# Logits of four tiles at once, second-half tiles stored turned, routing counts later, four residual additions on GpSimd

## The chip, the cores and the metric

The kernel runs on one core of a Trainium2 chip. The metric is the device time of one execution in microseconds. Before the change three runs took 824.46, 827.03 and 829.4 us; the median is 827.03 us.

## What is computed

The input is 2 x 1024 tokens of 512 numbers. Two residual blocks follow one another, each as `x + layernorm(f(layernorm(x)))`. The first f is attention (local windows, and global rows for the 62 largest queries and the two end tokens of each head). The second is a mixture of experts over all T = 2048 tokens, and this is the part that the change touches:

```
xt = layernorm(x).reshape(T, 512)
probs = softmax(xt @ Wg)                  # 8 experts
eidx = argmax(probs); gate = probs[eidx]
oh = one_hot(eidx, 8)
pos = (cumsum(oh, axis=0) * oh).sum(-1) - 1
keep = pos < 256                          # capacity
xd[eidx * 256 + pos] = xt                 # where keep
h = silu(xd @ W1) * (xd @ W3); oe = h @ W2          # per expert, H = 704
out = take(oe, ...) * (gate * keep)
shared = silu(xt @ sw1) * (xt @ sw3) @ sw2
x = x + layernorm(out + shared)
```

## The kernel before

Tokens are worked on in 16 tiles of 128. Matrix products in fp32 accuracy are made of a high and a low part of each operand (`split`, L169: a copy to the high part, on ScalarE, and a subtraction for the low part, on VectorE, `tt` L149) and three matmuls (`product3`, L286). The program builds one list of instructions for each engine, and each engine runs its list in order; semaphores tie them together. The order of the calls in the Python code is therefore the order in every list. SyncE issues most DMAs, also in order; indirect DMAs stand in GpSimd's list, between its arithmetic.

After the attention comes a list of passes (L1481): two of the shared expert for tokens 0 to 1023 (q = 0 and 1, 512 tokens each), eight experts (q = 2 to 9, 256 rows each), and two of the shared expert for tokens 1024 to 2047 (q = 10 and 11). A pass has `up` (L1324) with six blocks m = 0 to 5 (24 matmuls each, 12 in the last) and `down` (L1358), in which tiles 0 and 1 go through m = 0 to 5 as a pair and then tiles 2 and 3. A `step(m)` is called behind each block of `up`, and `between(t0, m)` behind each block of `down`. PSUM banks of `up` come from a ring of four (`UP`), those of `down` from a ring of two (`DN`), which ScalarE empties into `OUTR` (L1382). The logits use a single bank (`MSC`).

**Second layernorm and routing.** `work()` (L1556) is one step n of a software pipeline over the tiles. In step n it calls, for the tile that many steps back, `h_logits` (5 back, the matmuls with Wg), `h_turn` (4 back: four transposes on TensorE, then a copy or a split), `h_h2` (3 back: L934 on VectorE, then an activation on ScalarE), `h_mean2` (2 back), `h_x1` (1 back, with an addition on GpSimd at L874) and `h_mean` (0 back). Both means end in a power on GpSimd (L284). Step 7 stands ahead of q = 0, steps 8 to 12 behind its blocks m = 0 to 4, steps 13 to 15 in its `down`, steps 16 to 21 behind the blocks of q = 1. When four tiles have logits, `route_count` (L1416, 12 to 14 small VectorE operations) runs in the same step, right behind the logits and ahead of the step's other functions; one step later `route_place` (L1446) makes eight small matmuls, nine small VectorE operations and four indirect scatters on GpSimd into `scr_xd`. The experts' passes read `scr_xd` back in `prepare` (L1484), turn the rows on TensorE (`turned`, L915) and split them.

**Logits.** For tiles 0 to 7 `h_logits` makes eight matmuls per tile, with the turned 128 x 128 tile as the stationary operand and Wg (high and low, 16 columns) as the moving one. For tiles 8 to 15 it makes four matmuls in plain fp32 (eight records in the trace), with 8 columns.

**Second half.** `h_h2` stores the rows of tiles 8 to 15 to `scr_h` (`h2d`), and `prepare` loads them before q = 10 and 11 and turns them: four transposes a tile, at blocks m = 2 to 5 of q = 9 and q = 10.

**Last additions.** In q = 10 and 11, `step(m)` calls `conclude(m - 2)` (L1543: a tensor_scalar, the residual addition and the store of the result), then `combine(m - 1)` (L1531: a scalar_tensor_tensor of the gathered expert row and the shared row, then the statistics and GpSimd's power), then `fetch(m)` (L1512: an indirect gather on GpSimd and two loads). Tiles 0 to 3 are concluded in q = 10, tiles 4 to 7 in q = 11, tiles 8 to 15 at the ends of the two.

## Time and profile before

| | |
|---|---|
| median of three runs | 827.03 us (824.46 to 829.4) |
| the profiled execution, its own time | 822.52 us |
| its span, first to last instruction | 820.8 us |
| TensorE busy | 776.2 us (95%) |
| VectorE busy | 563.0 us (69%) |
| ScalarE busy | 422.9 us (52%) |
| GpSimd busy | 146.1 us (18%) |
| mean granted clock of TensorE | 0.992 of 2.4 GHz |

In the rows, PE is TensorE, DVE VectorE, ACT ScalarE, POOL GpSimd, SPq the DMA queue of SyncE. A row of the timeline has the start in us from the start of the span, the duration, the engine, the source line, the operation and output<-inputs; in brackets stands how long the engine was idle before it and what it waited for. XT, WQL and WKL hold turned tiles (WQL and WKL are old weight buffers used again), SIL and HH the hidden layer, STC the statistics of a tile, LG the routing's small operands, XX and CX the residual and the shared row. Small helpers (L145, L149, L163, L167) carry most operations, so tiles tell them apart.

### The profile page before, as it was taken

How to read it: one execution, taken by the hardware profiler on the slowest of the kernel's cores; microseconds unless marked ns; L12 is line 12 of the kernel's file. 1: busy time of each engine (PE TensorE's matmuls, PEld its weight loads, DVE VectorE, ACT ScalarE, POOL GpSimd, SP SyncE). 2: the span in 40 equal slices, each digit the busy share in tenths (PEclk: the TensorE clock that was granted, in tenths of full speed). 3: DMA queues.
4: the chain of work that ended last, by engine and by line, in shares of the span. 5: the costliest groups of instructions: out<-in, count | busy, mean ns of one | idle time of the engine just before them, and what ended most of it. 6: DMA issues, size and time to landing. Idle time of an engine off the chain costs nothing.

```text
span 820.8 us, 13876 instructions
## 1 busy us (share of the span) xinstructions
PE 776.2 (95%) x5060; PEld 650.2 (79%) x5060; DVE 563.0 (69%) x1196; ACT 422.9 (52%) x839; POOL 146.1 (18%) x227
## 2 busy tenths in 40 slices
PE   6998999989999999998999999999999999999994
PEld 4786777777777777776878887999999999887883
DVE  5764798468888566777588545466776666758666
ACT  5464352445656565767544244566675666633120
POOL 3300010510111113332354432000000000013122
PEclk9999999999999999999999999999999999999998
DMA  7789565976775888872349622676778776546444
GB/s 233 230 275 346 167 187 168 276 199 174 190 202 156 204 215 234 230 198 92 105 149 312 233 98 94 186 230 200 219 237 237 227 237 221 171 146 204 138 155 141
DMA packets 117492, 162.39 MB, mean 198 GB/s; under 512 B 17364, under 2 KB 65236, under 8 KB 117424
## 3 DMA queue, kind: packets, MB, share of 16 engines
q1 hardware_dynamic: 113840, 153.54, 61.9%
q0 software_dynamic: 3584, 7.97, 3.3%
q8 instruction: 40, 0.66, 0.4%
q14 instruction: 28, 0.23, 0.1%
HBM read 107.24 MB, written 55.05 MB: 198 GB/s over the span
## 4 chain that ended last, share of the span: by engine, by line
PE 63%; DVE 19%; DMA 6%; ACT 5%; issue 4%; SPq 1%; POOL 1%; POOLq 0%; DVEq 0%; ACTq 0%
PE bank L163 40%; PE wide L163 17%; DVE MX L160 4%; PE wide L167 3%; PE bank L167 2%; DVE SG L160 2%; DMA XX<-scr_xd 2%; DMA scr_q<-hl 1%; DVE STC L281 1%; ACT PTG L145 1%; DVE GC L153 1%; DMA H2A<-scr_oe,FG 1%; DMA scr_qtok<-H2A 1%; DVE TV L744 1%; ACT PT L157 1%
## 5 line engine op out<-in xcount | busy, mean ns | idle before, releaser
L163 PE MATMUL wide<-W2H,HH 128*128 128x512 f32 x308 | 101.9, 396 | 0.5 <-ACT OUTR L145 0.5
L160 DVE TENSOR_REDUCE MX<-wide 128x1 f32<-128x192 f32 (+1 forms) x128 | 77.6, 646 | 19.4 <-PE wide L163 19.3
L157 ACT ACTIVATE PT<-bank 128x512 f32<-128x512 f32 x128 | 73.6, 593 | 28.5 <-PE bank L163 28.4
L157 ACT ACTIVATE SIL<-bank 128x256 f32<-128x256 f32 (+1 forms) x72 | 32.7, 454 | 97.8 <-PE bank L163 97.6
L149 DVE TENSOR_TENSOR SIL<-bank,SIL 128x256 f32<-128x256 f32 (+1 forms) x72 | 36.8, 511 | 63.8 <-ACT SIL L157 63.2
L163 PE MATMUL bank<-XT,W13H 128*128 128x256 f32 (+1 forms) x336 | 76.6, 322 | 0.0
L145 ACT ACTIVATE HH<-SIL 128x256 fp32r<-128x256 f32 (+1 forms) x72 | 35.2, 489 | 67.5 <-DVE SIL L149 67.5
L163 PEld LDWEIGHTS wide<-W2H,HH 128*128 128x128 f32 x308 | 58.5, 190 | 13.2 <-ACT OUTR L145 1.3
L149 DVE TENSOR_TENSOR HH<-SIL,HH 128x256 fp32r<-128x256 f32 (+1 forms) x72 | 37.0, 514 | 45.5 <-ACT HH L145 37.3
L163 PE MATMUL wide<-W2L,HH 128*128 128x512 f32 x168 | 66.6, 396 | 0.9 <-DVE W2L L149 0.7
L163 PEld LDWEIGHTS bank<-XT,W13H 128*128 128x128 f32 x336 | 55.0, 188 | 4.7
L163 PE MATMUL bank<-WQL,W13H 128*128 128x256 f32 (+1 forms) x168 | 55.3, 329 | 0.0
L163 PE MATMUL bank<-WQL,W13L 128*128 128x256 f32 (+1 forms) x168 | 54.3, 323 | 0.0
L163 PE MATMUL bank<-WKL,W13H 128*128 128x256 f32 (+1 forms) x168 | 54.3, 323 | 0.0
L284 POOL TENSOR_TENSOR STC<-STC,mhalf 128x1 f32<-128x1 f32 x48 | 29.0, 604 | 138.4 <-DVE STC L153 135.1
L163 PE MATMUL bank<-XT,W13L 128*128 128x256 f32 (+1 forms) x168 | 53.6, 319 | 0.0
L1516 POOL DMA_INDIRECT H2A<-scr_oe,FG x8 | 8.0, 997 | 210.7 <-issue 210.7
L149 DVE TENSOR_TENSOR W13L<-R,W13H 128x512 fp32r<-128x512 f32 x70 | 44.1, 685 | 1.7 <-ACT W13H L145 1.7
L163 PE MATMUL bank<-XT,WQH 128*128 128x256 f32 (+1 forms) x192 | 43.0, 319 | 0.0
L163 PE MATMUL bank<-WVH,HT 128*128 128x512 f32 x128 | 41.1, 410 | 1.0 <-ACT HT L145 0.7
L149 DVE TENSOR_TENSOR W2L<-R,W2H 128x512 fp32r<-128x512 f32 x60 | 41.2, 686 | 1.3
L163 PE MATMUL bank<-HT,WKH 128*128 128x512 f32 x128 | 41.1, 402 | 0.0
(253 smaller groups left out, 2007.5 us busy)
## 6 DMA issues: line engine op xcount, KB each, us to landing
R<-in_L_ffn_W_dram SPq DMA_DIRECT2D x48, 512.0 KB, 5.5
scr_q<-hl SPq DMA_DIRECT2D x16, 512.0 KB, 4.3
scr_k<-hl SPq DMA_DIRECT2D x16, 512.0 KB, 4.1
R<-in_L_ffn_sw_dram SPq DMA_DIRECT2D x12, 512.0 KB, 5.3
QSe<-scr_q SPq DMA_DIRECT2D x36, 128.0 KB, 3.6
KSe<-scr_k SPq DMA_DIRECT2D x36, 128.0 KB, 3.0
scr_v<-vt SPq DMA_DIRECT2D x16, 272.0 KB, 2.2
R<-_attn_hidden_states_dram SPq DMA_DIRECT2D x16, 256.0 KB, 3.8
```

The costliest lines, as they stand in the source:

```text
L145: return do(e, lambda g: g.activation(dst, src, ACT.Copy), after)
L149: return do(e, lambda g: g.tensor_tensor(dst, a, b, op), after)
L153: return do(e, lambda g: g.tensor_scalar(dst, a, s1_, None, op0), after)
L157: return do("act", lambda g: g.activation(dst, src, fn, **kw), after)
L160: return do("dve", lambda g: g.tensor_reduce(dst, src, AXX, op), after)
L163: return do("pe", lambda g: g.matmul(ps, a, b, start=start, stop=stop, skip_group_check=True), after, mark=mark)
L167: return do("pe", lambda g: g.transpose(ps, a, idn), after, mark=mark)
L281: a = do("dve", lambda g: g.bn_stats(st[:, 8:14], src), after)
L284: return do("pool", lambda g: g.tensor_tensor(st[:, 2:3], st[:, 3:4], mhalf[:, :], ALU.pow), [a, m_half])
L744: m = do("dve", lambda g: g.max(v8, N_[:, :]), prev)
L1516: mg = dma("pool", ga_slots[i], lambda e: e.indirect_dma_start(out=gb, out_offset=None, in_=oed, in_offset=bass.IndirectOffsetOnAxis(ap=FG ...
```

## The change

- For tiles 0 to 7 the logits are made by `logits_group`: eight matmuls for four tiles, with Wg's 16 columns stationary and 512 tokens moving, into a bank of `UP`; ScalarE copies the 16 x 512 result to a buffer of `XL`. `logits_fold`, later, adds high and low part and turns the result back with four plain fp32 matmuls (16 rows, 8 columns), into `MSC`. The ScalarE copy and the VectorE addition at the head of `route_count` become one VectorE copy.
- Groups stand in steps 7 and 12, folds in step 8 and behind block m = 5 of q = 0. Counts: in step 8 behind the other functions, behind m = 5 of q = 0, and in steps 16 and 20, behind the others. Places: step 10, at (0, 3) in `down` of q = 0, step 18, and behind m = 5 of q = 1.
- `down` of q = 0 holds four steps (13 to 16, at (0, 1), (0, 4), (2, 1), (2, 4)) where it held three; q = 1 holds steps 17 to 21 behind m = 0 to 4.
- Tiles 8 to 15 are stored to `scr_h` after their turn, from `XL`, so `prepare` only loads and splits them for q = 10 and 11; no transposes there. A buffer of `XL` (two) is free again when that store has landed.
- In `conclude` the residual addition of tiles 0 to 3 goes to GpSimd.

```diff
+                            m_wg.append(tt(fold[:, :], ident[0:2 * E, 0:E], ident[0:2 * E, E:2 * E], ALU.add, [m_id]))
@@ h_h2: the store of tiles 8 to 15 goes
-            if t >= 8:
-                r0 = (t - 8) * P
-                m = dma("sp", h2s[t % 2], lambda g: g.dma_start(h2d[r0:r0 + P, :], dst),
-                        [m_h] + h2_marks[-2:-1])
-                h2_marks.append(m)
-                h2free[t % 8].append(m)
@@ h_turn, tiles 8 to 15
+                r0 = (t - 8) * P
+                m = dma("sp", h2s[t % 2], lambda g: g.dma_start(
+                    h2d[r0:r0 + P, :], d["dst"][:, :, :].rearrange("p k t -> p (k t)")), d["s"] + h2_marks[-2:-1])
+                h2_marks.append(m)
+                XL.busy[d["li"]].append(m)
@@
+            def logits_group(g4):
+                ui, ps, fr = UP.take()
+                li, lt, lf = XL.take()
+                x_ = xt[g4]
+                for l in range(2):
+                    for k in range(4):
+                        m_l = mm(ps[0:2 * E, :], wghl[:, k, :, :].rearrange("p l e -> p (l e)"),
+                                 x_["b"][l][:, k, :], k + l == 0, k + l == 4, x_["ready"] + m_wg + fr, mark=(k == 3 and l == 1))
+                XT.busy[x_["i"]].append(m_l)
+                m_c = copy("act", lt[0:2 * E, :, :].rearrange("p k t -> p (k t)"), ps[0:2 * E, :], [m_l] + lf)
+                UP.busy[ui].append(m_c)
+                route["lt"] = (li, lt, m_c)
+
+            def logits_fold():
+                li, lt, m_c = route["lt"]
+                route["mi"], route["mb"], fr = MSC.take()
+                for j in range(4):
+                    m_l = mm(route["mb"][:, j * 16:j * 16 + E], lt[0:2 * E, j, :], fold[:, :], True, True,
+                             [m_c] + m_wg + fr, mark=(j == 3))
+                XL.busy[li].append(m_l)
+                route["m_l"] = m_l
@@ route_count
-                if g4 < 2:
-                    a = copy("act", LG[:, 0, :, :], lg[:, :, 1, :], [m_l, m_cum])
-                    a = tt(LG[:, 1, :, :], lg[:, :, 0, :], LG[:, 0, :, :], ALU.add, [a])
-                else:
-                    a = copy("dve", LG[:, 1, :, :], lg[:, :, 0, :], [m_l, m_cum])
+                a = copy("dve", LG[:, 1, :, :], lg[:, :, 0, :], [m_l, m_cum])
@@ prepare
-                    m_t, s = turned(xb, d_["b"], (n - 2) * P, [m_], d_["free"], TPC)
-                    XX.busy[xi].append(m_t)
+                    c = (n - 2) * P
+                    if job < 9:
+                        m_t, s = turned(xb, d_["b"], c, [m_], d_["free"], TPC)
+                        XX.busy[xi].append(m_t)
+                    else:
+                        s = split(d_["b"][0][:, :, c:c + P], d_["b"][1][:, :, c:c + P],
+                                  xb[:, :].rearrange("p (k t) -> p k t", k=4), "act", [m_] + d_["free"])
+                        XX.busy[xi] += s
@@ conclude
-                m_f = tt(xb[:, :], xb[:, :], cb, ALU.add, [m_n, mx_])
+                m_f = tt(xb[:, :], xb[:, :], cb, ALU.add, [m_n, mx_], e="pool" if t < 4 else "dve")
@@ work
+            PLACE_AT = {10: 0, 18: 2}
                 if n == 7:
-                    h_logits(0)
-                    h_logits(1)
+                    logits_group(0)
+                if n == 8:
+                    logits_fold()
+                if n == 12:
+                    logits_group(1)
                 for back, fn in ((5, h_logits), (4, h_turn), (3, h_h2), (2, h_mean2), (1, h_x1), (0, h_mean)):
                     t = n - back
-                    if 4 <= t < 16 or 0 <= t < 4 and fn is h_logits:
+                    if (8 if fn is h_logits else 4) <= t < 16:
                         fn(t)
-                        if fn is h_logits and t % 4 == 3:
-                            route_count(t // 4)
-                if n % 4 == 1 and 9 <= n <= 21:
-                    route_place(n // 4 - 2)
+                if n in (8, 16, 20):
+                    route_count((n - 8) // 4)
+                if n in PLACE_AT:
+                    route_place(PLACE_AT[n])
@@ step
-                    if q == 1 or q == 0 and m < 5:
+                    if q == 0 and m == 5:
+                        logits_fold()
+                        route_count(1)
+                    if m < 5 and q < 2:
                         work()
+                    if q == 1 and m == 5:
+                        route_place(3)
@@ between
-                        if q == 0 and (t0, m) in ((0, 2), (2, 0), (2, 4)):
+                        if q == 0 and (t0, m) in ((0, 1), (0, 4), (2, 1), (2, 4)):
                             work()
+                        if q == 0 and (t0, m) == (0, 3):
+                            route_place(1)
```

## Rows read from the trace of the kernel before

**Rows 1.** The page: busy time, share of the span and instructions

```profile
PE 776.2 (95%) x5060; PEld 650.2 (79%) x5060; DVE 563.0 (69%) x1196; ACT 422.9 (52%) x839; POOL 146.1 (18%) x227
```

**Rows 2.** Timeline of TensorE: its longer idle times in brackets

```profile
171.91 0.48 PE L163 MATMUL bank<-QSe,KSe 97*128 97x256 f32 x2 [1.11 <-DVE vt L149]
...
412.83 1.03 PE L163 MATMUL wide<-wghl,XT 128*128 128x16 f32 x8 [1.02 <-DVE STC L934]
...
449.50 0.50 PE L163 MATMUL wide<-W2H,HH 128*128 128x512 f32 x1 [0.23 <-ACT OUTR L145]
...
497.66 0.18 PE L163 MATMUL bank<-OHB,trib 128*128 128x8 bf16 x1 [0.73 <-DVE OHB L146]
498.55 0.18 PE L163 MATMUL bank<-CUMB,onesb 128*128 128x8 bf16 x1 [0.71 <-DVE CUMB L146]
...
754.62 0.47 PE L163 MATMUL wide<-W2L,HH 128*128 128x512 f32 x1 [0.70 <-DVE W2L L149]
```

**Rows 3.** Windows: busy us per engine, then PEclk, DMA share, GB/s

```profile
410.00:420.00 10.00, 8.98 (x46) 7.18 (x45) 8.80 (x28) 4.18 (x8) 2.54 (x3) 0.83 0.26 86
500.00:510.00 10.00, 9.77 (x36) 7.56 (x35) 6.87 (x20) 6.35 (x11) 4.42 (x4) 0.83 0.13 45
```

**Rows 4.** Chain that ended last: start, us; 24 logit matmuls, 24 of block 0

```profile
396.85 2.63 PE wide L163 x24
399.49 5.58 PE bank L163 x24
```

**Rows 5.** Timeline of VectorE, q = 0: blocks' first operations, L934, place, count

```profile
405.72 0.69 DVE L149 TENSOR_TENSOR SIL<-bank,SIL 128x512 f32<-128x512 f32 x1 [5.05 <-ACT SIL L157]
...
415.14 0.68 DVE L149 TENSOR_TENSOR SIL<-bank,SIL 128x512 f32<-128x512 f32 x1
...
419.61 0.15 DVE L934 SCALAR_TENSOR_TENSOR STC<-STC 128x1 f32<-128x1 f32 x1
...
422.14 0.18 DVE L149 TENSOR_TENSOR LG<-bank,LG 128x32 f32<-128x32 f32 x1
...
423.67 0.68 DVE L149 TENSOR_TENSOR SIL<-bank,SIL 128x512 f32<-128x512 f32 x1
...
440.02 0.18 DVE L149 TENSOR_TENSOR LG<-wide,LG 128x32 f32<-128x32 f32 x1
...
442.44 0.15 DVE L934 SCALAR_TENSOR_TENSOR STC<-STC 128x1 f32<-128x1 f32 x1
```

**Rows 6.** Timeline of ScalarE: the activation behind L934

```profile
448.07 0.82 ACT L157 ACTIVATE H2A<-XX,STC 128x512 f32<-128x512 f32 x1 [0.47 <-DVE STC L934]
```

**Rows 7.** End of q = 1: first load of expert rows, their transposes, landing time

```profile
511.40 0.80 SPq L1503 DMA_DIRECT2D XX<-scr_xd  x2
...
515.53 1.03 PE L167 MATMUL wide<-ident,XX 128*128 128x128 f32 x8
...
XX<-scr_xd SPq DMA_DIRECT2D x3, 256.0 KB, 3.5
```

**Rows 8.** Chain that ended last: a tile's transposes; a combine and the next gather

```profile
743.43 0.44 PE wide L167 x4
...
783.96 0.76 DVE CX L1535
...
786.67 3.40 DMA H2A<-scr_oe,FG
```

**Rows 9.** Timeline of VectorE, q = 10: residual addition and two combines

```profile
735.90 0.69 DVE L149 TENSOR_TENSOR XX<-XX,CX 128x512 f32<-128x512 f32 x1
736.51 0.75 DVE L1535 SCALAR_TENSOR_TENSOR CX<-H2A,GK,CX 128x512 f32<-128x512 f32 x1
...
742.85 0.75 DVE L1535 SCALAR_TENSOR_TENSOR CX<-H2A,GK,CX 128x512 f32<-128x512 f32 x1
```

**Rows 10.** Timeline of GpSimd and VectorE: an addition, a one-column operation beside it

```profile
458.15 1.26 POOL L149 TENSOR_TENSOR XX<-XX,CX 128x512 f32<-128x512 f32 x1
458.21 1.22 DVE L934 SCALAR_TENSOR_TENSOR STC<-STC 128x1 f32<-128x1 f32 x1 [3.62 <-POOL STC L284]
```

More of the change, by code:

```diff
@@ L180, in sandwich @@
         wghl = sb(top, "wghl", [P, 4, 2, E], F32R)
+        fold = sb(top, "fold", [2 * E, E])
         wt8 = sb(top, "wt8", [P, E])
@@ L1393, in sandwich @@
             scat = []
+            def logits_group(g4):
[18 more added lines that the diff above has]
+                route["m_l"] = m_l
             def h_logits(t):
-                g4, j = divmod(t, 4)
+                j = t % 4
                 d = hs[t]
@@ L1399, in h_logits @@
                     route["mi"], route["mb"], route["mfree"] = MSC.take()
-                mb, dst = route["mb"], d["dst"]
-                if g4 < 2:
-                    col = d["col"]
-                    for k in range(4):
-                        for l in range(2):
-                            m_l = mm(mb[:, j * 16:(j + 1) * 16].rearrange("p (l e) -> p l e", l=2),
-                                     dst[l][:, k, col:col + P], wghl[:, k, :, :], k == 0 and l == 0,
-                                     k == 3 and l == 1, d["s"] + m_wg + route["mfree"], mark=(k == 3 and l == 1))
-                    XT.busy[xt[g4]["i"]].append(m_l)
-                else:
-                    for k in range(4):
-                        m_l = mm(mb[:, j * 16:j * 16 + E], dst[:, k, :], wgs[:, k, :], k == 0, k == 3,
-                                 d["s"] + m_wg + route["mfree"], mark=(k == 3))
-                    XL.busy[d["li"]].append(m_l)
+                for k in range(4):
+                    m_l = mm(route["mb"][:, j * 16:j * 16 + E], d["dst"][:, k, :], wgs[:, k, :], k == 0, k == 3,
+                             d["s"] + m_wg + route["mfree"], mark=(k == 3))
+                XL.busy[d["li"]].append(m_l)
                 route["m_l"] = m_l
@@ L1419, in route_count @@
                 lg = mb[:, 0:64].rearrange("p (j l e) -> p j l e", j=4, l=2)
-                if g4 < 2:
-                    a = copy("act", LG[:, 0, :, :], lg[:, :, 1, :], [m_l, m_cum])
-                    a = tt(LG[:, 1, :, :], lg[:, :, 0, :], LG[:, 0, :, :], ALU.add, [a])
-                else:
-                    a = copy("dve", LG[:, 1, :, :], lg[:, :, 0, :], [m_l, m_cum])
+                a = copy("dve", LG[:, 1, :, :], lg[:, :, 0, :], [m_l, m_cum])
                 L = LG[:, 1, :, :]
```

## The prediction

> **What bounds the kernel now.** I read the page first: TensorE is busy 95% of the span [rows 1], so a matmul taken away pays unless another wait takes its place. Then TensorE's idle times behind the attention [rows 2]: the large ones are 1.02 us in block 1 of q = 0, 0.73 + 0.71 us at the end of q = 1 (both behind a count on VectorE) and 0.70 us in q = 10. Then windows [rows 3]: after each of the first two the granted clock averages 0.83 over 10 us, which is about 3.4 us at 1.2 GHz instead of 2.4 and costs 1.7 us. Idle times of 1.11 us earlier [rows 2] brought no such drop. Last the timeline of VectorE in q = 0 [rows 5]: its list fills each step of 7.0 us, in which TensorE has some 6.9 us to do. So in q = 0 VectorE is a second bound, just hidden. The profiled run took 822.52 us and the median is 827.03; I sum changes against the profiled run and add the sum to the median. A measurement here can tell about 0.5% (4.1 us) from no change.
>
> **Logits, TensorE.** A tile's eight matmuls now cost 2.63 / 3 = 0.88 us [rows 4]; eight tiles cost 7.0 us. After: a 512-column matmul takes 5.58 / 24 = 0.23 us [rows 4], so a group costs 1.9 us. No row has stationary operands of 16 columns; if they don't pipeline, up to 0.40 us each (the time of one such matmul), 1.4 us more a group; I take 0.23, since the load is smaller. The fold (four plain fp32 matmuls, two records each) has no row either: between almost nothing and the time of eight small matmuls, 8 x 0.11 = 0.9 us [rows 4]; I take 0.9, the nearest. Sum 5.6 us, a gain of 1.4 us of TensorE time. It is worth that only where TensorE sets the pace.
>
> **q = 0, step by step, against VectorE.** The group ends 0.8 us earlier than the 24 matmuls, so block 0's first VectorE operation comes at 404.9 instead of 405.72 [rows 5]. A step without count or place lasts 415.14 to 422.14 = 7.0 us; a place 1.5 us (422.14 to 423.67), a count 2.4 us (440.02 to 442.44) [rows 5]. L934 of the next tile stands 4.5 us behind the step's start (415.14 to 419.61), and the tile can be turned 1.0 us later, after 0.82 us of ScalarE [rows 5, 6]. The count is now behind the other functions, so tile 5 is no longer late: the wait of 1.02 us goes. But step 9 starts on VectorE only at 404.9 + 7.0 + 2.4 = 414.3, and tile 6 can be turned at 414.3 + 4.5 + 1.0 = 419.8. TensorE, without logits, is there at 417.0 (404.1, then 0.9 fold, two turns of 0.4 [rows 8] and two blocks of 5.6). What is late next is this: 2.8 us idle. The same list gives 1.0 us before tile 7 and 0.9 us before the second group, which needs tile 7's split (433.7). Group, turn, half block and fold then end at 439.7.
>
> Then the moved count. Each 128x512 operation fewer saves 0.6 us (735.90 to 736.51) [rows 9]: one W13L in block 3, two and the XT split in block 4. So its steps end at 436.2 and 441.4, block 5 takes 2.8, and count 1 starts at 444.2. The logits of tile 8 (step 13, now at (0, 1), 442.5) need the one MSC bank, which is free when the count has read it, 0.4 us later: 2.1 us idle. TensorE then reaches the end of (0, 5) at 452.1. In ScalarE's list the step moved to (0, 4) stands ahead of the copy OUTR that frees the `down` bank: turned copy of tile 10 at 451.9, H2A 0.8 us, OUTR 0.6 us (448.07 to 449.50 for both now) [rows 2, 6], so TensorE starts the second pair at 453.3, 1.2 us idle. Before it started at 449.50 with one step (1.2 us) less done [rows 2]: 450.7. **q = 0 loses 2.6 us.** Bounds: a gain of 4.1 us (1.4 work, 1.0 idle, 1.7 clock) if VectorE doesn't hold it, a loss of 5 if each wait is 0.6 us longer. Step 16's matmuls only move from q = 1 to q = 0. The four scatters of a place and GpSimd's power stay in the same order as before and cover step 15 as before.
>
> **End of q = 1.** Count 3 comes a block earlier and its place two blocks later: 1.44 us idle and 1.7 us of clock go. But q = 2 needs rows scattered by place 3. The first VectorE operation of block 5 was held to 498.5 by the count where its input was there at 497.6 (TensorE ended at 496.93); this 0.9 us is all that the scatters gain. The load issued at 511.40 lands 3.5 us later, at 514.9, and was used at 515.53 [rows 7]: 0.6 us slack. **Gain 1.5 us** of 3.1; bounds 0.9 and 3.1. The other 1.6 us become idle time before those transposes.
>
> **Turned stores.** The stores move one function ahead in SyncE's list and wait for a copy instead of an activation of the same step; same bytes. The buffer of XL, then, waits for its store, two steps (over 9 us) old: nothing, or up to 1 us a step if the store is late. Loads for q = 10 and 11 stay, splits read the loaded buffer (same lengths). Four transposes a tile take 0.44 us [rows 8]: **q = 9 gains 1.8 us** on TensorE; those in q = 10 would give another 1.8 and the idle 0.70.
>
> **Additions on GpSimd.** VectorE loses 0.69 us a tile [rows 9], GpSimd gets 1.26 [rows 10]. In q = 10 combine follows combine after 6.34 us [rows 9]; without the addition VectorE would be back after 5.65, but the next gather lands 6.11 us after a combine (783.96 to 790.07) [rows 8]. So the combine waits, GpSimd's addition starts first, and the combine meets it: beside such an addition a one-column VectorE operation with two SBUF inputs took 1.22 us and ended with it, against 0.15 alone [rows 10, 5]. The combine starts at 5.65 + 0.1 (a semaphore) + 1.26 = 7.0 us, 0.65 later than now; twice that, less the first addition's 0.6: W2L of block 5 comes 0.7 us later than now. TensorE then waits 2.9 us there instead of 0.70: **q = 10 loses 0.7** and its 1.8 us of transposes with it. Bounds: -2.5 and +1.3.
> The Trainium skill (SBUF — State Buffer, "Who interferes with whom") says that an instruction with two SBUF inputs and a GpSimd instruction that reads SBUF exclude each other, and that the later one stands still; by it q = 10 loses 0.7, and without it the combine would wait for the gather alone, and q = 10 gain 1.0. The rows agree with the rule; it speaks against this part.
>
> **Clock.** New idle times of 2.8 and 2.1 us in q = 0 and 2.9 us in q = 10 are longer than the one of 1.02 that brought 1.2 GHz [rows 2, 3]. A drop after the first is hidden by VectorE; I count one of the other two, 1.7 us; bounds 0 and 3 drops, 5.1.
>
> **Sum:** 2.6 - 1.5 - 1.8 + 0.7 + 1.7 = +1.7 us; 824.2 against the profiled 822.52, 828.7 against the median.
>
> **Rivals.**
> - *TensorE sets the pace everywhere* (chance 0.10): -4.1 - 1.5 - 1.8 - 2.5 = -9.9, 817.1. For it: 95% busy. Against it: rows 5 and the gather.
> - *Only q = 0 goes as TensorE would* (0.13): -4.1 - 1.5 - 1.8 + 0.7 = -6.7, 820.3. The waits there rest on sums over some 40 us.
> - *The combine beats the addition* (0.14): q = 10 gains 1.0 instead of losing 0.7: 0.0, 827.0. It would need a gather 0.5 us faster.
> - *Slower: the clock drops after each new idle time* (0.20): in the second half of `down` in q = 0, at the start of q = 2 and in q = 10, +5.1 instead of +1.7, so 832.1. It decides where the idle time passes about the 1.02 us of rows 2. For it: both late cases dropped. Against it: 1.11 us earlier did not.
> - *The weights aren't held* (0.03): 0.40 us a matmul, +2.8, mostly under VectorE: about 830.
>
> **How the numbers follow.** My forecast has 0.40: 828.7. Faster by over 0.5%: the first two rivals and little else, 0.25. Slower: the clock rival and a fifth of the forecast's error, 0.25. Same: 0.50. The range, 819.5 to 833.5, takes in the second rival and the clock, and leaves out TensorE everywhere.
>
> **What would show it.** Right: idle of TensorE near 417, 442 and 452 us, the last two put down to MSC's reader and OUTR; no idle at a count's OHB or CUMB; no transposes from scr_h; L1535 lasting or starting late beside GpSimd's additions in q = 10, and W2L idle there over 2 us. Wrong: `down` of q = 0 starting before 438; combines 5.7 us apart in q = 10; a span under 815 us.

## The result and the profile after

The changed kernel takes 829.68 us (median of 20 runs, 826.7 to 836.03), the kernel before 825.2 us (20 runs, the three shown first among them, 821.32 to 829.4): a ratio of 1.0061, 95% interval 1.0044 to 1.0078, so 5.0 us slower. Ratios here are worked out from the single runs, slow ones left out, and can differ by about a per mille from the quotient of the two medians (here 1.0054). The time itself lies 1 us from the forecast of 828.7 and inside the range. The difference does not: I had summed +1.7 us, and my likeliest case was "within 0.5%", where the middle of the interval is beyond 0.5%. (The kernel before is 1.8 us faster in the 20 runs than in the three shown first; that covers part of my miss. It is luck and no merit of the forecast.)

The page of the changed kernel, the line that answers to [rows 1]. TensorE is busy as long as before, although 64 matmul records are gone (more of it ran at half clock, see below); the span is 829.3 us against 820.8:

```profile
PE 777.0 (94%) x4996; PEld 645.9 (78%) x4996; DVE 563.3 (68%) x1193; ACT 423.5 (51%) x839; POOL 150.9 (18%) x231
```

Timeline of TensorE, changed kernel, all the longer idle times behind the attention, for [rows 2]:

```profile
422.63 0.66 PE L167 MATMUL wide<-ident,H2B 128*128 128x128 f32 x4 [3.08 <-ACT H2B L157]
...
442.02 1.12 PE L167 MATMUL wide<-ident,H2A 128*128 128x128 f32 x4 [3.22 <-ACT H2A L157]
...
452.13 1.03 PE L163 MATMUL wide<-wgs,XL 128*128 128x8 f32 x8 [0.19 <-DVE LS L160]
...
461.27 0.51 PE L163 MATMUL wide<-W2H,HH 128*128 128x512 f32 x1 [0.94 <-ACT OUTR L145]
...
522.92 1.33 PE L167 MATMUL wide<-ident,XX 128*128 128x128 f32 x8 [0.16 <-DMA XX<-scr_xd]
...
719.74 0.47 PE L163 MATMUL wide<-W2L,HH 128*128 128x512 f32 x1 [0.75 <-ACT W13H L145]
...
761.81 0.77 PE L163 MATMUL wide<-W2L,HH 128*128 128x512 f32 x1 [3.61 <-DVE W2L L149]
```

The two idle times at a count's OHB and CUMB are gone. In their place stand three of over 3 us: at tile 6 (422.63), at tile 8 (442.02), and at W2L in q = 10 (761.81). The windows behind them, changed kernel, with the columns of [rows 3]; the granted clock is the first number behind POOL's:

```profile
424.00:428.00 4.00, 4.00 (x13) 3.15 (x12) 3.20 (x8) 2.68 (x5) 1.35 (x2) 0.61 0.55 180
440.00:448.00 8.00, 5.97 (x17) 4.60 (x17) 4.39 (x11) 4.22 (x7) 2.24 (x4) 0.57 1.09 366
760.00:764.00 4.00, 2.19 (x5) 1.82 (x6) 2.94 (x6) 0.69 (x2) 2.60 (x3) 0.70 0.48 139
```

A stretch at a clock of 0.61 for 4 us has cost 4 x 0.39 = 1.6 us of TensorE's time at full speed; the second has cost 8 x 0.43 = 3.4 us. Over the whole span the granted clock cost the kernel before 6.7 us in this way and the changed one 11.6; 3.3 and 3.1 us of that lie in the last 15 us of the span, and 1.7 us of the changed one in the attention.

**Where the time went, by stage.** The starts of the first matmul of each `up` and `down` (for q = 0 the first matmul of the logits ahead of it) cut the span in stages. The row "before" has lengths; the others are differences from it, in us. The kernels e1 to e12 are those of the next section. The last stage is taken from a span with one decimal and is good to 0.1 us.

```
kernel   attention  q=0 up  q=0 down  q=1 up  q=1 down  q=2..8    q=9  q=10 up  q=10 down  q=11 down on  span
                                                                                 + q=11 up
before      396.66   42.88     20.44   38.76     19.47  171.12  25.37    32.15      47.02         26.93  820.8
after        +2.31   +7.08     +2.34   -3.00     -1.21   -0.55  -0.93    -1.66      +4.33         -0.21  829.3
e1           +0.82   +1.63     +5.39   -2.99     -1.19   -0.32  -0.91    -1.64      +4.78         +0.03  826.4
e2           +0.57   +1.10     +4.09   -3.00     -1.14   -0.39  -0.93    -1.64      +4.38         +0.16  824.0
e3           -0.65   +4.00     +4.03   -3.00     -1.11   -0.55  -0.94    -1.66      +1.62         -0.94  821.6
e4           +0.61   +3.21     -0.24   +0.01     -0.03   -0.65  -0.94    -1.65      +1.93         -0.55  822.5
e5           +7.90   +5.17     -0.30   +0.04     -1.64   -0.51  +1.47    +0.02      +2.76         +0.39  836.1
e6           +5.24   +1.58     +1.81   -3.00     +0.17   -0.62  -0.08    +0.00      +0.01         +0.19  826.1
e7           +3.79   +5.01     +1.19   -2.99     -1.14   +0.76  -0.94    -1.65      +1.65         -0.78  825.7
e8           +2.69   -1.20     -0.23   +0.00     -1.47   -0.86  +0.40    +0.01      -0.01         +0.17  820.3
e9           +0.16   +5.94     +2.54   -2.99     -0.66   -0.31  -0.94    -1.64      +3.00         +0.70  826.6
e10          -0.63   +4.34     +4.02   -3.00     -1.23   -0.57  -0.94    -1.65      -0.24         -1.30  819.6
e11          +1.62   -0.01     +1.80   -3.03     +0.12   -0.37  -0.94    -1.65      -0.22         -1.32  816.8
e12          +5.84   +3.15     +1.10   -2.80     -1.64   -0.15  -0.93    -1.65      -0.26         -0.76  822.7
```

The attention is the same code in all of them, and so are q = 2 to 8: these columns, from -0.65 to +7.90 and from -0.86 to +0.76, are what one profiled execution can be off by. The profiles of e5 and e12 are of the slowest of their runs. I compare the other stages and trust the medians for the whole. The ratios have intervals of about 2.5 per mille to either side, so a difference of less than 3 to 4 per mille between two of them is not firm. For the changed kernel: q = 0 costs 9.4 us more, q = 1 4.2 us less (1.2 us of that is the step moved to q = 0), q = 2 to 9 1.5 us less, q = 10 and what follows 2.5 us more.

**What holds tile 8.** ScalarE's timeline in the changed kernel, and GpSimd's, the scatter of tile 0:

```profile
441.16 0.81 ACT L157 ACTIVATE H2A<-XX,STC 128x512 f32<-128x512 f32 x1 [5.64 <-DMA scr_xd<-H2A,FSI]
```

```profile
433.38 1.04 POOL L1478 DMA_INDIRECT scr_xd<-H2A,FSI  x1 [1.02 <-DVE SIL L149]
```

Tile 8's rows go into the buffer of tile 0 (`h2_tile(t)` goes by t % 8), so the activation waits until the scatter of tile 0 has read it. Place 0 moved from step 9 to step 10; the scatter was issued at 424.40 before and at 433.38 now, and among the weight loads of block 3 it took until 441.1, 7.7 us (6.1 us before). I had not followed this edge.

**q = 10.** VectorE's and GpSimd's timelines in the changed kernel, for [rows 9]:

```profile
741.82 0.75 DVE L1551 SCALAR_TENSOR_TENSOR CX<-H2A,GK,CX 128x512 f32<-128x512 f32 x1
...
749.44 0.75 DVE L1551 SCALAR_TENSOR_TENSOR CX<-H2A,GK,CX 128x512 f32<-128x512 f32 x1 [1.93 <-DMA H2A<-scr_oe,FG]
...
755.57 1.43 DVE L1551 SCALAR_TENSOR_TENSOR CX<-H2A,GK,CX 128x512 f32<-128x512 f32 x1 [0.49 <-DMA H2A<-scr_oe,FG]
```

```profile
741.99 1.73 POOL L149 TENSOR_TENSOR XX<-XX,CX 128x512 f32<-128x512 f32 x1 [3.08 <-DVE CX L154]
...
755.16 1.29 POOL L149 TENSOR_TENSOR XX<-XX,CX 128x512 f32<-128x512 f32 x1 [2.02 <-DVE CX L154]
```

The exclusion is there in both directions: at 741.82 the combine starts first and GpSimd's addition takes 1.73 us instead of 1.26 [rows 10]; at 755.57 the addition is under way and the combine takes 1.43 us and ends half a microsecond after it. The combines come 7.6 and 6.1 us apart. The same pair (an addition of 1.73 us, a combine of 1.43 to 1.50 us) is in e1, e2 and e9, which keep this order of calls, and in no kernel with another.

### The profile page after: what moved, and what is told of

The parts are those of the page before. It is cut to its first block and busy times, and to the rows that moved or that the text cites. A ratio compares the mean times of both kernels' runs of the same rounds, so it can differ in the third digit from the quotient of the medians.

```text
span 829.3 us, 13764 instructions
## 1 busy us (share of the span) xinstructions
PE 777.0 (94%) x4996; PEld 645.9 (78%) x4996; DVE 563.3 (68%) x1193; ACT 423.5 (51%) x839; POOL 150.9 (18%) x231
```

## The experiments

My theory after reading the traces: q = 0 lost by the scatter of tile 0 and by VectorE's list, q = 10 by the gather and the exclusion. Rivals: TensorE's work decides; the clock decides; VectorE is full whatever the order. All ratios are to the kernel before, run beside.

**e1: place 0 back in step 9.**

```diff
-            PLACE_AT = {10: 0, 18: 2}
+            PLACE_AT = {9: 0, 18: 2}
```

> The changed kernel with one edit: the place of tiles 0 to 3 goes back from step 10 to step 9, as it was before the change. In the changed kernel ScalarE's activation of tile 8 (into the buffer of tile 0) waited 5.64 us for the scatter of tile 0, and TensorE then 3.22 us for tile 8; about 3 us at half clock followed. Theory A (the moved place is what q = 0 lost): the scatters are issued some 7 us earlier, ahead of the weight loads of block 3, land in 3.5 to 6 us, the wait at 441 us and the TensorE idle of 3.22 us go, and the time falls by 3 to 5 us against the changed kernel, to the time of the kernel before within 2 us. Rival B (VectorE's list holds q = 0 anyway): the 1.5 us of the place fall into the step that already carries the late count, tile 6 or 7 is turned 1.5 us later, and the time falls by less than 1.5 us. Rival C (the half clock is the loss and comes after any idle): the idle near 442 goes, the drop stays, the gain is about 2 us.

Measured: 829.47 us against 825.8, ratio 1.0042 (1.0022 to 1.0062). The wait of tile 8 is gone, but TensorE now waits for the late count instead. Its timeline in e1:

```profile
414.89 0.18 PE L163 MATMUL bank<-OHB,trib 128*128 128x8 bf16 x1 [2.39 <-DVE OHB L146]
415.77 0.18 PE L163 MATMUL bank<-CUMB,onesb 128*128 128x8 bf16 x1 [0.71 <-DVE CUMB L146]
```

It took 1.9 per mille less time than the changed kernel (1.6 us, not firm): not the 3 to 5 us of theory A, nearer to rival B. A count behind the functions of step 8 can't have its place in step 9 without TensorE paying 3.1 us; the change had a reason for moving the place.

**e2: the weight loads two blocks later.**

```diff
@@ step, q == 0
-                        else:
-                            for g3 in range(3):
-                                load_13(1, g3)
                     if q == 0 and m == 5:
+                        for g3 in range(3):
+                            load_13(1, g3)
                         logits_fold()
```

> The changed kernel with one edit: the loads of expert 0's first weights go from behind block 3 of q = 0 to behind block 5, so that they no longer run beside the scatters of tiles 0 to 3. Theory A with transfers in each other's way: the scatters land in 3.5 to 6 us instead of 6.5 to 7.7, the wait of tile 8's activation falls from 5.6 us to about 3, TensorE's idle near 442 us from 3.2 to about 1, and the time falls by 2 to 4 us. Rival (a scatter takes what it takes, and the weights have no part in it): landing times and idle stay, the time moves by less than 1 us.

Measured: 826.95 us against 825.8, ratio 1.0022 (0.9995 to 1.0049), 3.9 per mille or 3.2 us less than the changed kernel. In e2 tile 8's activation no longer waits at all:

```profile
440.22 0.81 ACT L157 ACTIVATE H2A<-XX,STC 128x512 f32<-128x512 f32 x1
```

and the median time of the eight scatters from H2A (four of place 0, four of place 2) fell from 4.6 to 2.7 us (the page's list of DMA issues, changed kernel and e2):

```profile
scr_xd<-H2A,FSI POOLq DMA_INDIRECT x8, 4.6
```

```profile
scr_xd<-H2A,FSI POOLq DMA_INDIRECT x8, 2.7
```

The four of place 0 alone took 7.7, 7.4, 7.0 and 6.5 us in the changed kernel and 3.1, 2.7, 2.7 and 2.8 us in e2; those of place 2 did not change. Theory A holds: the scatters of 256 KB each ran beside six weight loads, and that was the wait. The loads now run beside the scatters of place 1, which take 6.1 to 6.7 us instead of 2.7 to 3.8; no engine was seen waiting for those. What was late next is what I had predicted ahead of the change, the bank of the logits behind count 1; the changed kernel hid it (0.19 us at 452.13), e2 shows it:

```profile
446.15 1.03 PE L163 MATMUL wide<-wgs,XL 128*128 128x8 f32 x8 [1.88 <-DVE LS L160]
```

**e3: the four additions back on VectorE.**

```diff
-                m_f = tt(..., ALU.add, [m_n, mx_], e="pool" if t < 4 else "dve")
+                m_f = tt(..., ALU.add, [m_n, mx_], e="dve")
```

> The changed kernel with the four residual additions back on VectorE. Theory (the exclusion between GpSimd's addition and the combine delays W2L in q = 10): TensorE's idle at W2L in q = 10 falls from 3.61 us to under 1.5, the half clock behind it goes, combines come 6.3 us apart, and the time falls by 2 to 4 us. Rival (the gathers set the distance of the combines, so the engine of the addition does not matter): the idle at W2L stays over 2.5 us and the time moves by less than 1 us.

Measured: 827.19 us against 825.8, ratio 1.0022 (1.0003 to 1.004), 3.2 us less. The stage of `down` in q = 10 (with `up` of q = 11) takes 2.7 us less, and no half clock follows. The idle at W2L fell only to 2.46 us, not under 1.5: the combines are 6.27 us apart, and none of them waits for its gather, so this is VectorE's own list in a pass whose block takes TensorE 5.6 us. Timeline of TensorE in e3:

```profile
756.40 0.47 PE L163 MATMUL wide<-W2L,HH 128*128 128x512 f32 x1 [2.46 <-DVE W2L L149]
```

**e4: the turned stores alone, on the kernel before.**

```diff
@@ h_h2
-            if t >= 8:
...
-                m = dma("sp", h2s[t % 2], lambda g: g.dma_start(h2d[r0:r0 + P, :], dst),
@@ h_turn
+                m = dma("sp", h2s[t % 2], lambda g: g.dma_start(
+                    h2d[r0:r0 + P, :], d["dst"][:, :, :].rearrange("p k t -> p (k t)")), d["s"] + h2_marks[-2:-1])
@@ prepare
+                    if job < 9:
+                        m_t, s = turned(xb, d_["b"], c, [m_], d_["free"], TPC)
...
+                    else:
+                        s = split(d_["b"][0][:, :, c:c + P], d_["b"][1][:, :, c:c + P],
```

> The kernel before with the turned stores alone (no transposes for tiles 8 to 15 in q = 9 and q = 10, additions on VectorE, logits and counts as before). Theory (q = 10 is held by VectorE's additions and combines, q = 9 by TensorE): q = 9 gains 1.8 us, q = 10 turns its 1.8 us into idle time at W2L (0.7 to about 2.5 us), and the time falls by 1.8 us against the kernel before, more if the half clock stays away. Rival (TensorE alone sets the pace): it falls by 3.6 to 4.3 us. Rival (the store from XL holds a buffer too long, or the stores collide with loads): q = 1 shows idle time at the logits of tiles 10 to 15, and the time does not fall.

Measured: 827.01 us against 825.8, ratio 1.0021 (0.9998 to 1.0043): no gain, where the theory had 1.8 us less. By stage it does what the theory says from q = 9 on: -0.94, -1.65, +1.93, -0.55, so -1.2 us. That q = 0 took 3.0 us more in this profile is not its doing by any edge I can find: its extra there is half clock at 401 to 404 and again behind an idle time of 1.28 us that e12 shows too and e11, with the same stores, does not. TensorE's waits at the logits of tiles 5 and 7 in e4:

```profile
415.12 1.03 PE L163 MATMUL wide<-wghl,XT 128*128 128x16 f32 x8 [1.03 <-DVE STC L934]
...
430.71 1.03 PE L163 MATMUL wide<-wghl,XT 128*128 128x16 f32 x8 [1.28 <-DVE STC L934]
```

In e4 and e12 no half clock followed the wait at tile 5, and TensorE waited at tile 7; in the kernel before, e6 and e11 it ran at half clock behind tile 5 and did not wait at tile 7. The half clock takes the place of that wait, as VectorE's list is the later of the two there. The 3.0 us are this wait of 1.28 us and the half clock at 401 (1.7 us). Why the median of e4 shows no gain stays open. q = 9 gains 0.94 instead of 1.8, because the last block there now waits for ScalarE's splits (the row at 719.74 above, 0.75 us, is the same in e4).

**e5: the groups alone, on the kernel before.**

```diff
+                if n == 7:
+                    logits_group(0)
+                if n == 8:
+                    logits_fold()
+                    route_count(0)
+                if n == 12:
+                    logits_group(1)
                 for back, fn in ((5, h_logits), (4, h_turn), (3, h_h2), (2, h_mean2), (1, h_x1), (0, h_mean)):
...
+                if n == 12:
+                    logits_fold()
+                    route_count(1)
```

> The kernel before with the logits of tiles 0 to 7 in groups of four and folded, and nothing else: counts 0 and 1 in steps 8 and 12 (count 0 ahead of the step's other functions, count 1 behind them, since its fold needs ScalarE's copy), places in steps 9 and 13, no change elsewhere. TensorE has 1.4 us less to do in q = 0. Theory (VectorE's list holds q = 0): the block part of q = 0 stays within 1 us of the kernel before, and the saved TensorE time is found as idle time at the turns of tiles 5 to 8; the time stays within 1.5 us. Rival (TensorE holds q = 0, and the loss of the full change comes from where it puts counts and places): q = 0 gets 1.4 us shorter and the time falls by 1.4 to 2.5 us.

Measured: 832.79 us against 828.18, ratio 1.0042 (1.0011 to 1.0073). Slower, which neither side had: the saved TensorE time comes back as idle time and more. Timeline of TensorE in e5:

```profile
421.06 1.03 PE L167 MATMUL wide<-ident,H2B 128*128 128x128 f32 x4 [1.93 <-ACT H2B L157]
...
436.67 0.66 PE L167 MATMUL wide<-ident,GC 128*128 128x128 f32 x4 [1.52 <-ACT GC L157]
...
447.19 1.05 PE L163 MATMUL wide<-fold,XL 16*128 16x8 f32 x8 [1.98 <-ACT XL L145]
```

5.4 us of idle time in q = 0, with two drops of the clock, where the kernel before has 1.02 us and one. The third is new in kind: the group's result passes through ScalarE, whose copy (XL, at 446.57) stands in its list behind the splits and activations of its step, and the fold stands waiting for it at the head of TensorE's.

**e6: the second half of the moves alone, on the kernel before.**

```diff
-                        if fn is h_logits and t % 4 == 3:
-                            route_count(t // 4)
-                if n % 4 == 1 and 9 <= n <= 21:
-                    route_place(n // 4 - 2)
+                        if fn is h_logits and t in (3, 7):
+                            route_count(t // 4)
+                if n in (16, 20):
+                    route_count((n - 8) // 4)
+                if n in (9, 13, 18):
+                    route_place({9: 0, 13: 1, 18: 2}[n])
@@ step
-                    if q == 1 or q == 0 and m < 5:
+                    if m < 5 and q < 2:
                         work()
+                    if q == 1 and m == 5:
+                        route_place(3)
@@ between
-                        if q == 0 and (t0, m) in ((0, 2), (2, 0), (2, 4)):
+                        if q == 0 and (t0, m) in ((0, 2), (2, 0), (2, 2), (2, 4)):
```

> The kernel before with only the second half of the moves: four steps (13 to 16) in the down part of q = 0 instead of three, counts 2 and 3 behind the functions of steps 16 and 20, place 2 in step 18 and place 3 behind block 5 of q = 1. Logits, counts 0 and 1, stores and additions as before. Both traces put the idle of 0.73 + 0.71 us and the half clock behind it at the end of q = 1 to the late count, and the runs of the full change so far finish q = 1 in 4.1 us less than before, of which 1.2 us is the step moved to q = 0. Theory: q = 1 takes 4.1 us less, q = 0 1.2 us more, and the time falls by 2 to 3.5 us. Rival (the step moved to q = 0 brings its own wait at OUTR and at the bank of the logits): the down part of q = 0 takes over 3 us more and the time falls by less than 1 us.

Measured: 827.76 against 828.18, ratio 0.9988 (0.996 to 1.0016). q = 1 takes 2.8 us less and the step in q = 0 costs 1.8: a gain of 1.0 us, not 2 to 3.5 (the median can't tell it from none). Part of the gain turned into this, the row I had predicted (timeline of TensorE in e6):

```profile
521.24 1.29 PE L167 MATMUL wide<-ident,XX 128*128 128x128 f32 x8 [1.58 <-DMA XX<-scr_xd]
```

**e7: e4, e5 and e6 together, additions on VectorE.** The diff is the sum of theirs.

> The kernel before with the groups of e5, the turned stores of e4 and the early last counts of e6; counts 0 and 1 and places 0 and 1 stay in steps 8, 12, 9 and 13, additions on VectorE. If the parts add up as their own runs show (turned stores 0 to +1.7 us in the median, groups within 1.5, early counts -2 to -3.5), the time is 2 to 4 us below the kernel before. Rival (moved idle times bring the half clock, so that gains of one part are lost at the next): it is within 1.5 us of the kernel before or above it.

Measured: 828.48 against 828.18, ratio 0.9993 (0.9961 to 1.0025): the rival. q = 0 costs 6.2 us, of it 1.93, 1.49 and 1.98 us idle as in e5; q = 1, q = 9 and q = 10 give it back. The rival was right in the number and not in its reason: between the attention and the end half clock cost e7 3.4 us, as much as the kernel before. What took the gains was idle time in q = 0.

**e8: one logit matmul for a tile.**

```diff
-                    for k in range(4):
-                        for l in range(2):
-                            m_l = mm(..., dst[l][:, k, col:col + P], wghl[:, k, :, :], ...)
+                    m_l = mm(..., dst[0][:, 0, col:col + P], wghl[:, 0, :, :], True, True, ...)
```

> The kernel before with one logit matmul for each of tiles 0 to 7 instead of eight; the other seven products of the logits are left out, so that the routing goes by other numbers. TensorE has 7/8 of 7.0 = 6.2 us less to do in q = 0. It bounds what any cheaper way to the logits can bring. Theory (VectorE holds q = 0): 1.3 us of this falls ahead of block 0 and is gained at most in part, the rest turns into idle time at the turned tiles; q = 0 gains under 2.5 us and the time falls by 1 to 2.5 us. Rival (TensorE holds q = 0): q = 0 gains 5 us or more.

Measured: 824.53 against 828.18, ratio 0.9959 (0.9932 to 0.9985), 3.4 us less. In the profile q = 0 takes 1.4 us less for 6.2 us less work, and TensorE waits where the work was:

```profile
413.66 0.25 PE L163 MATMUL wide<-wghl,XT 128*128 128x16 f32 x1 [2.27 <-DVE STC L934]
414.48 0.66 PE L167 MATMUL wide<-ident,H2B 128*128 128x128 f32 x4 [0.58 <-ACT H2B L157]
...
421.49 0.66 PE L167 MATMUL wide<-ident,H2B 128*128 128x128 f32 x4 [0.46 <-ACT H2B L157]
...
429.26 0.25 PE L163 MATMUL wide<-wghl,XT 128*128 128x16 f32 x1 [1.53 <-DVE STC L934]
430.08 0.99 PE L167 MATMUL wide<-ident,GC 128*128 128x128 f32 x4 [0.57 <-ACT GC L157]
```

5.4 us idle in five places. So VectorE's list holds q = 0, and no way of making these logits, however cheap on TensorE, was worth more than some 3 us (5.6 at the edge of the interval); the one that saves 1.4 us was worth nothing (e5). The whole gained 3.4 us, somewhat more than the 2.5 that the theory allowed; in the profile q = 1 is 1.5 us shorter too, as the half clock at its end did not come this time.

**e9: the waits filled.**

```diff
+        def filler(n):
+            ti, tb, tf = TPC.take()
+            for i in range(n):
+                m_t = tr(tb[:, 0:P], ident[:, :], ident[:, :], tf, mark=(i == n - 1))
+            TPC.busy[ti].append(m_t)
@@ h_turn
+            if t in (6, 8):
+                filler(24)
@@ down of q = 10, behind (0, 4)
+                            filler(28)
```

> The changed kernel, with TensorE kept working where it waited longest: 24 transposes of the identity (some 2.6 us, results unused) ahead of the transposes of tile 6 and of tile 8 in q = 0, and 28 (3.1 us) ahead of W2L of block 5 in q = 10. In the changed kernel the waits there were 3.08, 3.22 and 3.61 us, and 4.2, 3.4 and 2.7 us at half clock (lost: 1.9, 3.4 and 1.7 us) followed. Theory (the half clock is brought by the idle time itself and is a cost of its own): the waits shrink to under 1 us each, no half clock follows them, no work comes later than before, and the time falls by 3 to 6 us against the changed kernel, 1.5 to 3 us if the clock is hidden by VectorE in q = 0. Rival (the drops come with something else, as the work of VectorE or a budget of the chip): they stay, and the time is the same or higher by up to 1 us.

Measured: 829.6 against 823.91, ratio 1.0078 (1.005 to 1.0106): no gain, if not a loss. Timeline of TensorE in e9, tile 6, and W2L:

```profile
419.67 4.15 PE L167 MATMUL wide<-ident 128*128 128x128 f32 x24 [2.26 <-DVE STC L943]
```

```profile
759.76 0.47 PE L163 MATMUL wide<-W2L,HH 128*128 128x512 f32 x1 [0.78 <-DVE W2L L149]
```

At tile 6 the filler waited itself, since it writes the bank that tile 5's split still read (the row names the VectorE operation right behind that split), and then ran at half clock in TensorE's way: that third is a failed experiment. At tile 8 and at W2L the waits were filled and no half clock followed. The stage of `down` in q = 10 took 1.3 us less than in the changed kernel. But e3's 2.62 and 2.46 us there brought no drop either, so this supports the link without showing it, and here it brought no gain of the whole.

**e10: another order in the steps of q = 10 and 11.**

```diff
-                        if 0 <= m - 2 < 4:
-                            conclude(t0 + m - 2)
+                        if m < 4:
+                            fetch(t0 + m, True)
                         if 0 <= m - 1 < 4:
                             combine(t0 + m - 1, None, [], lambda a: None)
-                        if m < 4:
-                            fetch(t0 + m, True)
-                        else:
+                        if 0 <= m - 2 < 4:
+                            conclude(t0 + m - 2)
+                        if m >= 4:
                             fetch(4 * g + 2 * m - 8, False)
```

> The changed kernel with the three calls in a step of q = 10 and q = 11 in another order: fetch, combine, conclude instead of conclude, combine, fetch. The gather is then issued ahead of the combine's power on GpSimd, so a combine no longer waits for it, and the addition on GpSimd starts behind the combine, beside VectorE's work on a PSUM operand. Theory (q = 10 lost by the gather and by the exclusion of GpSimd's addition and the combine): combines come 5.6 to 5.8 us apart instead of 7.6 and 6.1, the 1.93 us wait for the gather and the combine of 1.43 us go, TensorE's idle at W2L falls from 3.61 us to under 1.5, the half clock behind it goes, and the time falls by 3 to 5 us. Rival (VectorE is full there whatever the order): W2L stays idle over 2.5 us and the time falls by less than 1 us.

Measured: 823.25 against 823.91, ratio 0.999 (0.9969 to 1.0011); 7.1 per mille, 5.8 us, less than the changed kernel. VectorE and GpSimd in e10, and TensorE at W2L:

```profile
737.32 0.74 DVE L1551 SCALAR_TENSOR_TENSOR CX<-H2A,GK,CX 128x512 f32<-128x512 f32 x1
...
743.04 0.74 DVE L1551 SCALAR_TENSOR_TENSOR CX<-H2A,GK,CX 128x512 f32<-128x512 f32 x1
...
748.72 0.74 DVE L1551 SCALAR_TENSOR_TENSOR CX<-H2A,GK,CX 128x512 f32<-128x512 f32 x1
```

```profile
740.06 1.30 POOL L149 TENSOR_TENSOR XX<-XX,CX 128x512 f32<-128x512 f32 x1
...
745.77 1.27 POOL L149 TENSOR_TENSOR XX<-XX,CX 128x512 f32<-128x512 f32 x1
```

```profile
754.74 0.47 PE L163 MATMUL wide<-W2L,HH 128*128 128x512 f32 x1 [0.58 <-DVE W2L L149]
```

Combines 5.7 us apart, none waits, none is prolonged; the stage of `down` in q = 10 went from +4.33 to -0.24 us. The rival (VectorE full whatever the order) falls. Against e3, which has the additions on VectorE in the old order, e10 is 3.2 per mille faster, which is at the edge of what is firm. No run has the new order with the additions on VectorE, so what the order brings by itself is not separated; in e3 no combine waited for its gather, so at least that wait was not there to be removed.

**e11: the best mix.** The kernel before with the diffs of e4, e6 and e10, and the additions of tiles 0 to 3 on GpSimd; its own logits, counts 0 and 1 and places 0 and 1.

> The kernel before (its logits, its counts 0 and 1, its places 0 and 1) with the turned stores, the early last counts, and GpSimd's additions in the order of e10. Its parts by their own profiles: q = 1 minus 3.0, down part of q = 0 plus 1.2 to 1.8, q = 9 minus 0.9, up part of q = 10 minus 1.7, down part of q = 10 between 0 and plus 1 if the order of e10 works (plus 1.9 to 4.3 if not). Theory: 3.5 to 5 us below the kernel before. Rival (new idle times bring half clock at about 1.7 us each and take it back): within 1.5 us of the kernel before.

Measured: 818.91 against 823.91, ratio 0.994 (0.9918 to 0.9961): 5.0 us below the kernel before, at the upper end of what was expected and faster than both kernels. q = 0 keeps its length and pays 1.8 us for the step.

**e12: e11 with place 3 a block earlier.**

```diff
-                if n in (9, 13, 18):
-                    route_place({9: 0, 13: 1, 18: 2}[n])
+                if n in (9, 13, 18, 21):
+                    route_place({9: 0, 13: 1, 18: 2, 21: 3}[n])
-                    if q == 1 and m == 5:
-                        route_place(3)
```

> The mix of e11 with place 3 one block earlier, in step 21 instead of behind block 5 of q = 1. In e11 TensorE was idle 1.54 us ahead of the transposes of q = 2, which waited for the rows that place 3 scatters. Theory: count 3 is over on VectorE when block 4 ends (in e6, which has the same counts, CUMB was written at 501.30 us and TensorE ended block 4 at about 501.3), so the place's matmuls wait under 0.5 us, the scatters are issued 3 to 5 us earlier, the idle of 1.54 us goes, and the kernel is about 1 to 1.5 us faster than e11: 0.992 to 0.993 of the kernel before. Rival (the place's matmuls wait for the count as before the change): the idle comes back at OHB or CUMB with 0.7 us or more, and the time is that of e11 (0.994) or worse.

Measured: 819.72 against 825.05, ratio 0.9932 (0.9906 to 0.9958). The idle ahead of q = 2's transposes is gone and q = 1 takes 1.5 us less than in e11 (-4.4 against -2.9), as expected; the ratios of e11 and e12 overlap, so the median can't confirm it.

## Why the forecast of the time held and that of the difference did not

Step by step, in the order of the prediction.

- **Logits, TensorE: right.** A group takes 1.88 us (398.97 to the next block's 400.85), a fold 0.98 us (406.39 to 407.37); I had 1.9 and 0.9. The weights are held; that rival is out. The timeline of TensorE, changed kernel:

```profile
398.97 1.11 PE L163 MATMUL bank<-WQL,wghl 128*16 128x512 f32 x4
399.92 1.08 PE L163 MATMUL bank<-WKL,wghl 128*16 128x512 f32 x4
400.85 0.39 PE L163 MATMUL bank<-WQL,WQH 128*128 128x512 f32 x1
...
406.39 1.05 PE L163 MATMUL wide<-fold,XL 16*128 16x8 f32 x8
407.37 0.66 PE L167 MATMUL wide<-ident,H2B 128*128 128x128 f32 x4
```

- **q = 0 against VectorE: the frame right, the size wrong.** VectorE holds q = 0 (e8), and the idle time at tile 6 (3.08, I had 2.8), at the bank of the logits (1.88 in e2, I had 2.1) and at OUTR (0.94, I had 1.2) are where I put them. The 1.0 and 0.9 us at tile 7 and at the second group did not come; TensorE was at half clock behind tile 6 instead (1.7 us). The step that failed is the sentence on the scatters, "The four scatters of a place and GpSimd's power stay in the same order as before and cover step 15 as before". I looked at GpSimd's queue and not at who waits for the data: tile 8 waits for tile 0's scatter. It cost 3.22 us of idle time and 3.4 us of clock, of which the waits it covered (tile 7, the second group, the bank) gave some back. The stage lost 9.4 - 1.2 = 8.2 us where I had 2.6. With the scatters on time (e2) it lost 5.2 - 1.2 = 4.0, within my bound of 5.
- **End of q = 1: right.** Gain 1.5 of 3.1 us with 1.6 coming back as idle time before the transposes. e6 has 1.58 us there, and q = 1 with the moved step counted gains 2.83 - 1.2 = 1.6 us. The changed kernel did better, 3.0 us, as its idle time there is 0.16 us: its last scatter is followed by the load of the rows after 2.35 us (517.92 to 520.27) against 3.60 in e6 (514.83 to 518.43). Why the scatter lands sooner there stays open; the landing of that scatter takes 2.3 us in e7, e10 and also in e12, which has no groups, 2.8 in e9 and 3.4 in e11.
- **Turned stores: q = 9 wrong by half.** 0.93 us instead of 1.8 (q = 10's transposes gave 1.66 in `up` and were lost again in `down`, as said). The missed term is ScalarE: with TensorE 1.8 us earlier, the splits of the next weights are what is late (0.75 us). No wait of XL for its store was seen.
- **Additions on GpSimd: right.** I had q = 10 lose 0.7 us without the clock. It lost 4.33 - 1.66 - 0.21 = 2.5 us with 1.7 of clock, so 0.8. The combines came 7.6 and 6.1 us apart where I had 7.0 twice, and TensorE waited 3.61 us at W2L where I had 2.9. The exclusion rule that I cited (the Trainium skill, SBUF — State Buffer, "Who interferes with whom") is borne out by the combine of 1.43 us and the addition of 1.73.
- **Clock: too small.** I counted one drop; there were three places, two in q = 0 (the second twice as long) and one in q = 10. Leaving out the attention and the end of the span, the sum is 6.8 us (424, 440 and 760) against 3.4 (414 and 500) before: +3.4 us. The prediction counted new drops apart from the one behind tile 6, which it held to be hidden: of those there were 3.4 + 1.7 = 5.1 us where it had 1.7. That is the full price of the rival "the clock drops after each new idle time", at two places and not at its three.

Added up from the profiles, without the attention: q = 0 +8.2 (I had +2.6), q = 1 -3.0 (-1.5), q = 2 to 9 -1.5 (-1.8), q = 10 and behind +2.5 (+2.4 with the clock), together +6.2 where I had +1.7. q = 0 is the one part that was badly off.

So the changed kernel is 5.0 us slower and not 1.7, and the 3.3 us between are about what e2 took back by freeing tile 0's buffer in time (3.2 us, of which the two intervals leave some 2.6 us to either side): mainly one missed edge, paid in idle time and in clock.

## What to carry to other kernels

When a step is moved, follow the data of its DMAs as well as its queue: a buffer used again eight tiles later turns a later scatter into a wait two engines away, and big loads issued around it double its landing time (6.5 to 7.7 us against 2.7 to 3.1 here). Where a second engine is as full as TensorE, cheaper matmuls bring idle time and perhaps a lower clock, not time; here a cheaper version of the logits lost 0.4% by itself. When an operation is moved to GpSimd, look at what VectorE does beside it: the same four additions cost 3.2 us against VectorE in one order of three calls, and with the other order, which also issues the gathers earlier, the kernel was 5.8 us faster.

## What the runs showed of the hardware that I had not expected

- **For idle times of 1 to 3 us, their length did not tell whether the clock fell.** In the fourteen profiles, between the attention and the end, TensorE's idle times of 3.05 us and more were followed by half clock in 8 of 8 cases, those of 1.0 to 3.0 us in 14 of 30. The same idle time in the same place did either: 1.02 us at the logits of tile 5 was followed by it in the kernel before, e6 and e11, not in e12 (nor 1.03 in e4); 0.73 + 0.71 us at the last count was in the kernel before and e4, not in e5 and e8. Nor does each drop follow such an idle time: in e4, e6 and e12 the clock fell at 401, 405 and 406 us, 7 us or more behind an idle time of 0.33 us, the last one of over 0.1 us. What decides it stays open. Nearly each drop cost 1.7 us, the one at tile 8 twice that. That makes single profiles of this kernel differ by several microseconds (the attention's column above, and q = 0 of e4 and e12).
- **The scatter's time hangs on what runs beside it:** 256 KB took 2.7 to 3.1 us with the weight loads moved away (place 0 in e2) and 6.5 to 7.7 us among six of these loads (the changed kernel).
- **The exclusion works both ways:** whichever of GpSimd and VectorE starts second is held, GpSimd's addition too (1.73 us against 1.26).
